# One bias product for four query tiles in the cross-attention scores of a decoder layer

## The reference

```python
def _L0_xattn_ref(x, content_embeddings, Wq, bq, Wk, bk, Wv, bv, Wo, bo):
    queries = x @ Wq.T + bq
    keys = content_embeddings @ Wk.T + bk          # 77 rows in each batch
    values = content_embeddings @ Wv.T + bv
    scale = 1.0 / jnp.sqrt(jnp.asarray(C, x.dtype))
    scores = jnp.einsum('bqc,bkc->bqk', queries, keys) * scale
    attn = jax.nn.softmax(scores, axis=-1)
    attended = jnp.einsum('bqk,bkc->bqc', attn, values)
    out = x + attended
    return out @ Wo.T + bo

x = x + attn(layernorm(x));  x = x + xattn(layernorm(x), ctx);  x = x + ffn(layernorm(x))
```

## Time and profile before

| | before |
|---|---|
| median of three runs | 1726.41 us |
| the profiled execution, whole | 1725.03 us |
| its span | 1723.2 us |
| PE busy | 1625.2 us (94% of the span) |
| DVE busy | 1024.4 us (59%) |
| ACT busy | 787.4 us (46%) |
| granted TensorE clock, mean | 0.976 of full speed |

### The profile page before, as it was taken

The page is one execution under the profiler, slowest core; times in us unless marked ns, Lnnn a source line. Parts: engine busy times, 40 slices in busy tenths (PEclk is TensorE's granted clock), DMA queues, the critical chain, the costliest instruction groups (busy, mean ns, idle before and its releaser), DMA issues.

```text
span 1723.2 us, 29797 instructions
## 1 busy us (share of the span) xinstructions
PE 1625.2 (94%) x10070; PEld 972.2 (56%) x10070; DVE 1024.4 (59%) x2366; ACT 787.4 (46%) x1635; POOL 321.7 (19%) x310
## 2 busy tenths in 40 slices
PE   3689999999999999999999999799999999999996
PEld 1333333344444434445434443259999899999986
DVE  3488878788778788777788676323354332333322
ACT  2107666667655666655665657562222122122211
POOL 5301120001210050310031100412134122221221
PEclk8779999999999999999999999899999999999999
DMA  6640413331313440314422603234566765656663
GB/s 178 150 85 25 78 17 62 41 41 32 71 26 78 65 91 1 41 38 90 78 55 38 133 10 119 100 124 134 139 190 185 203 175 169 197 171 179 175 166 74
DMA packets 90837, 173.31 MB, mean 101 GB/s; under 512 B 12947, under 2 KB 47763, under 8 KB 90560
## 3 DMA queue, kind: packets, MB, share of 16 engines
q1 hardware_dynamic: 74272, 143.69, 33.0%
q0 software_dynamic: 15744, 26.54, 7.3%
q10 hardware_dynamic: 672, 1.18, 0.3%
HBM read 133.69 MB, written 37.29 MB: 99 GB/s over the span
## 4 chain that ended last, share of the span: by engine, by line
PE 89%; DVE 3%; ACT 3%; DMA 2%; issue 2%; POOL 0%; SPq 0%; ACTq 0%; POOLq 0%; DVEq 0%
PE ps L1181 14%; PE ps L979 14%; PE ps L1163 14%; PE ps L1000 14%; PE ps L965 12%; PE ps L1030 3%; ACT prob L1193 2%; DVE rmax L1328 2%; PE ps L1039 2%; PE ps L1083 2%; PE ps L1052 2%; PE ps L1003 2%; PE ps L1021 2%; PE ps L968 2%; PE ps L1151 1%
## 5 line engine op out<-in xcount | busy, mean ns | idle before, releaser
L1328 DVE TENSOR_REDUCE rmax<-ps 128x1 f32<-128x512 f32 x1024 | 665.8, 686 | 234.9 <-PE ps L1003 125.3
L1193 ACT ACTIVATE prob<-ps 128x512 f32<-128x512 f32 x1024 | 562.4, 601 | 363.1 <-PE ps L968 185.8
L1000 PE MATMUL ps<-stacked_k,stacked_q 112*128 112x512 bf16 x1024 | 396.5, 391 | 22.9 <-DMA stacked_k<-parts_of_rows 15.0
L965 PE MATMUL ps<-stacked_q,stacked_k 115*128 115x512 bf16 x1024 | 361.8, 384 | 15.7 <-issue 8.0
L979 PE MATMUL ps<-prob,values 128*32 128x512 f32 x2048 | 276.3, 612 | 7.4 <-ACT prob L1193 7.2
L1000 PEld LDWEIGHTS ps<-stacked_k,stacked_q 112*128 112x128 bf16 x1024 | 99.8, 98 | 301.7 <-DVE rmax L1328 201.2
L1163 PEld LDWEIGHTS ps<-xiT,w_now 128*128 128x128 f32 x2272 | 265.2, 192 | 3.7
L1181 PE MATMUL ps<-w,hidT 128*128 x1136 | 260.0, 382 | 7.7 <-issue 6.0
L1163 PE MATMUL ps<-xiT,w_now 128*128 128x128 f32 x2272 | 266.9, 275 | 0.0
L1297 ACT ACTIVATE hidT<-ps,b 128x128 f32<-128x128 f32 x284 | 81.1, 368 | 356.3 <-PE ps L1163 318.6
L1181 PEld LDWEIGHTS ps<-w,hidT 128*128 128x128 f32 x1136 | 210.1, 190 | 40.3 <-issue 14.4
(11 more groups left out here) (181 smaller groups left out, 1146.6 us busy)
## 6 DMA issues: line engine op xcount, KB each, us to landing
w_now<-in_w SPq DMA_DIRECT2D x71, 1024.0 KB
stacked_q<-parts_of_rows SPq DMA_DIRECT2D x96, 128.0 KB, 5.7
stacked_k<-parts_of_rows SPq DMA_DIRECT2D x93, 128.0 KB, 6.6
xi<-expert_rows SPq DMA_DIRECT2D x71, 130.0 KB, 2.1
w<-in_w SPq DMA_DIRECT2D x8, 1024.0 KB, 9.5
parts_of_rows<-q_part SPq DMA_DIRECT2D x24, 256.0 KB, 3.6
parts_of_rows<-k_part SPq DMA_DIRECT2D x21, 256.0 KB, 4.9
xr<-in_x POOLq DMA_DIRECT2D x4, 1024.0 KB, 9.1
```

What stands on the lines that cost most here:

```text
L965: m = e.matmul(ps[:, bank, :], ka[i][0:ROWS, hh, kt * P:(kt + 1) * P], qa[i][0:ROWS, hh, ch * BANK:(ch + 1) * BANK], start=True, stop=True)
L1000: m = e.matmul(ps[:, bank, :], qa[i][0:MAX_ROW, hh, qt * P:(qt + 1) * P], ka[i][0:MAX_ROW, hh, kc * BANK:(kc + 1) * BANK], start=True, sto ...
L1193: e.activation(prob[:, u % NPROB, :], ps[:, u % NSCORE, :], ACT.Exp).then_inc(sem["exp"], 1)
L1328: e.tensor_reduce(rmax[:, G % 2, hh * NT + qt, kc:kc + 1], ps[:, p.bank("max", *k), :], AX.X, ALU.max).then_inc(sem["maxed"], 1)
```

## The change

The bias is no longer added tile by tile. In the first part of a `cross` step one product, now line L1063, writes the bias of all four tiles to the 308 columns: the stationary operand is the same row of ones, and the moving operand is the row of 77 numbers, read four times over by a step of zero. The products of the keys (now L1067) then all add to what stands there. A batch's 8 tiles had 8 bias products and now have 2; the whole kernel had 32 of 77 columns, and now has 8 of 308. The number of products with keys stays at 64. The parts, their places in the order and the semaphores are as before.

```diff
                     bank = side_bank(kind, *k, first=first)
+                    if first:
+
+                        e.matmul(ps[:, bank, 0:4 * CTX], ones_row[:, :], ctx_bias[:, b, :].unsqueeze(1).broadcast_to([1, 4, CTX]), start=True, stop=True)
                     for q in (2 * part, 2 * part + 1):
                         tt, cols = 4 * four + q, slice(q * CTX, (q + 1) * CTX)
                         for c in range(DC):
-                            e.matmul(ps[:, bank, cols], xT[:, c, tt * P:(tt + 1) * P], ctx_keys[:, b, c, :], start=(c == 0), stop=False)
-                        m = e.matmul(ps[:, bank, cols], ones_row[:, :], ctx_bias[:, b, :], start=False, stop=True)
+                            m = e.matmul(ps[:, bank, cols], xT[:, c, tt * P:(tt + 1) * P], ctx_keys[:, b, c, :], start=False, stop=(c == DC - 1),
+                                         skip_group_check=True)
                     if final:
                         m.then_inc(sem["cross"], 1)
```

## The result

| | before | changed |
|---|---|---|
| median | 1727.61 us (6 runs, 1725.69 to 1731.1) | 1718.06 us (6 runs, 1716.25 to 1721.8) |
| ratio | | 0.9947, 95% interval 0.9931 to 0.9963 |
| profiled execution, whole | 1725.03 us | 1720.87 us |
| its span | 1723.2 us | 1719.0 us |

The change makes the kernel 0.53% faster: 9.2 us by the ratio (its interval allows 6.4 to 11.9), 9.55 between the medians. 8.7 us and 1717.7 us were forecast. The three runs before the forecast had a median of 1726.41 us, all six have 1727.61.

The account below looks back on a forecast made before the run. PE's own pace was taken to bound the kernel at the parts. Gains of 8.1 (second parts), 0.8 (first parts) and 0.2 us (followers) make 9.1, less 0.4 of waits: 1726.4 - 8.7 = 1717.7 us, range 1714.5 to 1723.

Parts of the forecast that it names:

- PE sets the time at the parts: Around the cross parts PE never waits while DVE and ACT stand idle 1.29 and 2.02 us, so shorter parts advance everything.
- A second part saves 1.01 us: Eight second parts lose both bias pairs and all switches: 0.94 us each for 1.95, 8.1 us in all.
- First parts save 0.8 us: Eight first parts swap two narrow bias pairs for one wide pair: 1.83 us for 1.95 behind a diagonal product.
- Followers, 0.2 us: Float32 products behind the last batch's four parts no longer follow a bias: four passes take 0.55 us, not 0.60.
- The pieces of a switch: At a one-row bias pair: 0.09 us lost going in, 0.10 coming out, exposed load 0.11; wide pair 0.73 us.
- Waits grow by 0.4 us: With PE earlier, its waits for ACT and DVE elsewhere grow, taking 0.4 us off the 9.1 us gain.
- The profiled execution, 1716.3 us: Whole kernel: the earlier profiled execution of 1725.0 us, less the 8.7 us gain, would take 1716.3 us.
- The signs: New profile shows: 16 bias passes near 0.42 us, key passes 0.11 apart, PE idle near 10 us, last third 7 earlier.
- Only the passes count: At the bias products, drains stay and only pass pace matters: gain 2.8 us, time 1723.6 us; 7 in 100.
- The slow zero step: At L1063 the four-times zero-step read is slow: gain only 3.1 us, time 1723.3 us; 4 in 100.
- Gain turned into waits: Behind the parts DVE or ACT becomes the bound, half of 9.1 us returns as waits: 1721.9 us; 8 in 100.
- Slower: Around 1100 to 1130 us ACT's unexplained stalls multiply, some 4.5 us each; four more give 1735.7 us; 4 in 100.

Follow-up runs that it names:

- the four experiments that vary its pieces: Four variants of the bias product: per tile with 128 rows, wide with 128 rows, one per part, four narrow in a row; ratios 0.9959, 0.9943, 0.998, 0.9977.
- the second one: Second profile of the changed kernel, run again with nothing altered; median 1716.74 us, ratio 0.9946 against the kernel before.
- the third profile of before: The unchanged kernel before, profiled a third time; 1731.39 us.
- the second experiment, full_each: Kernel before, still one bias product per tile, but its operands fill all 128 rows (identity times a row held by all partitions); median 1720.54 us, ratio 0.9959.
- on_dve: Kernel before with the bias products removed from PE; DVE adds the bias, held by all partitions, before the maximum; median 1709.65 us, ratio 0.99.
- the second of before: The unchanged kernel before, profiled a second time; 1730.94 us.

## Why the prediction was right

- **PE sets the time at the parts.** Right. DVE and ACT still wait for PE behind each part.
- **A second part saves 1.01 us.** Measured 0.99 (1.95 to 0.96; 2.06 to 1.07), 7.9 us in all where 8.1 was forecast. The key pass is 0.112 us, not 0.11.
- **First parts save 0.8 us.** Measured 0.14 in the two behind a diagonal product (forecast 0.12), 0.09 in the three behind 512 columns (0.07), 0.28 at 974 us (0.27), 0.08 in each of the last batch (0.05): 1.0 us.
- **Followers, 0.2 us.** The gain at the parts, 9.2, less the 8.9 of the parts, leaves 0.3.
- **The pieces of a switch.** 0.09 in, 0.10 out, an exposed load of 0.11: the wide pair measured 0.71 for 0.73, and the four experiments that vary its pieces came out within 0.3 us of sums made from them, at the parts.
- **Waits grow by 0.4 us.** Wrong, they did not grow; it took 0.4 from a sum that was right at 9.1 (9.2 measured).
- **The profiled execution, 1716.3 us.** Wrong: 1720.87. I took the one profile of before as typical. It was the fastest of three, 6 us under the others, mostly by its first 130 us; the changed kernel's profile in turn lies 2.8 us above that kernel's median.
- **The median, 1717.7 us, for 1718.06.** That it fits to 0.4 us is in part luck. The start, 1726.4, was 1.2 us below the median of all six runs, and the forecast gain, 8.7, was 0.85 us below the 9.55 between the medians; the two misses nearly cancel, and medians of this kernel scatter by more.
- **The signs.** The 16 bias passes average 0.469 us and not about 0.42. Parts and key passes came out as forecast, and PE's idle time from 130 to 1000 us stayed at 10.3 us. The last third did not start some 7 us earlier in the profile: at 1000 us it was 2.5 us earlier (4.7 in the second one), though the parts had given 6.9 by then, because the first 130 us came out longer and, in the first profile, the stretch behind the router too. Against the third profile of before it is 8.1 us.
- **Rivals.** Only the passes count: refuted by the second experiment. The rule behind this rival, that loads are pulled ahead (the Trainium skill, TensorE: Matmul & The Clock Gate, What happens when you issue a matmul), agrees with the trace where the rows are equal: the load of `ident` does go ahead, at 452.65 for 452.71. The load of the one row does not: 450.67 for 450.68. The slow zero step: no cost. Gain turned into waits: none. Slower: ACT's unexplained waits from 1060 to 1150 us were 10.5 us for 9.1, in two waits again, so the stall moved with the rest, and PE's starts from 1100 to 1165 us lost 0.3 us. Its line in the changed kernel:

```profile
ACT prob L1196 <- remote: 10.5, 2, 6.4
```

## What to carry to other kernels

On an engine that never waits, look at the distance of starts and not at busy time: the bias pairs looked like 14 us of busy PE and took 15.8 us with their ways in and out (the parts' 32.3 us less the 16.4 of on_dve), of which 8.7 us was switching (32.3 less the 23.6 of full_each). A float32 product with one row among products with 128 cost some 0.3 us more here than the same product with 128; give it full rows (the identity times a row held by all partitions), put several of them in a row, or let an engine with room do the addition. And where a change is worth 0.5%, align the starts of two traces stretch by stretch: that repeats to 0.1 us where executions scatter by 6.

## What the hardware showed beside that

The clock granted to PE fell to its lower level, 1.2 GHz, for a few us around the end of the router's narrow products (16 passes of 8 columns, twice) near 590 us in seven of the ten profiles, and not in the other three. From 585 to 600 us its mean was 0.77 in the changed kernel's profile and in the third of before, and 1.00 in the second of before, with the same work around it and PE busy for all 15 us. Between the second and the third of before this stretch moved 3.2 us. The first 130 us, in which PE waits for transfers (15.6 us for `xwo` in the first profile of before, 17.0 in the second), moved by up to 4.6 us more between profiles of the kernel before.
